# An attention block with adaptive layer norm: the order of the side work, one piece in each even step

## What is computed

```
h = _layernorm(x, axis=-1) * (1 + ca) + sa
x = x + ga * _L0_attn_ref(h, Wq, Wkv_down, Wk_up, Wv_up, Wo)
h = _layernorm(x, axis=-1) * (1 + cb) + sb
x = x + gb * _L0_ffn_ref(h, weight, disha)

# _L0_attn_ref(x):
q = (x @ Wq.T).reshape(b, t, N_HEADS, HEAD_DIM)
kv_latent = x @ Wkv_down.T
k = (kv_latent @ Wk_up.T).reshape(b, t, N_HEADS, HEAD_DIM)
v = (kv_latent @ Wv_up.T).reshape(b, t, N_HEADS, HEAD_DIM)
scores = jnp.einsum('bqhd,bkhd->bhqk', q, k) * scale
attn = jax.nn.softmax(scores, axis=-1)
out = jnp.einsum('bhqk,bkhd->bqhd', attn, v)
return out.reshape(b, t, N_HEADS * HEAD_DIM) @ Wo.T

# _L0_ffn_ref(x):
result = jnp.einsum('bsd,od->bso', x, weight)
pooled = x.reshape(*x.shape[:-1], x.shape[-1] // r, r).sum(axis=-2)
return result + pooled @ disha
```

## Time and profile before

| | us |
|---|---|
| median of 3 runs | 3562.01 (3559.07 to 3562.82) |
| profiled execution | 3557.84 |
| its span, first to last instruction | 3555.9 |
| PE busy | 3328.4 (94%) |
| POOL busy | 2510.2 (71%) |
| DVE busy | 2463.9 (69%) |
| ACT busy | 1672.1 (47%) |
| chain that ended last: PE, DVE, POOL, ACT | 74%, 9%, 6%, 3% |

### The profile page before, as it was taken

The page is one execution under the profiler, slowest core; times in us unless marked ns, Lnnn a source line. Parts: engine busy times, 40 slices in busy tenths (PEclk is TensorE's granted clock), DMA queues, the critical chain, the costliest instruction groups (busy, mean ns, idle before and its releaser), DMA issues.

```text
span 3555.9 us, 50728 instructions
## 1 busy us (share of the span) xinstructions
PE 3328.4 (94%) x14886; PEld 1920.0 (54%) x14886; DVE 2463.9 (69%) x2846; ACT 1672.1 (47%) x3075; POOL 2510.2 (71%) x1513
## 2 busy tenths in 40 slices
PE   5899999989999999999999999999999989999996
PEld 3444555545555564555646555464555645556454
DVE  4667767677676766767777676775767767676663
ACT  1444545444454444545444454544545445454443
POOL 1667677767776677667777677777777776777775
PEclk7999999999999999999999999999999999999998
DMA  1001010010101001010010100101010010100101
GB/s 56 30 24 51 22 59 20 28 49 30 52 19 62 21 25 51 28 55 19 31 50 22 60 20 28 48 31 52 19 62 19 28 53 24 54 25 28 36 30 33
DMA packets 98083, 129.34 MB, mean 36 GB/s; under 512 B 11121, under 2 KB 62449, under 8 KB 97777
## 3 DMA queue, kind: packets, MB, share of 16 engines
q1 hardware_dynamic: 97776, 125.64, 10.2%
...
## 4 chain that ended last, share of the span: by engine, by line
PE 74%; DVE 9%; issue 8%; POOL 6%; ACT 3%; DMA 0%; POOLq 0%; ACTq 0%; DVEq 0%; SPq 0%
PE ps_mix L544 22%; PE ps_max L587 12%; PE ps_score L565 12%; PE ps_score L567 10%; PE ps_side_b L532 5%; PE ps_side_b L649 5%; DVE neg_max L972 4%; POOL prob_sum L833 3%; PE ps_side_a L636 3%; PE ps_side_b L667 3%; DVE recip L952 2%; POOL x_in L852 1%; POOL rstd L819 1%; DVE h_lo L994 1%; ACT h_whole L772 1%
## 5 line engine op out<-in xcount | busy, mean ns | idle before, releaser
L833 POOL TENSOR_TENSOR prob_sum<-prob_sum,probs 128x1024 f32<-128x1024 f32 x768 | 1837.7, 2393 | 436.5 <-ACT probs L732 387.5
L972 DVE TENSOR_REDUCE neg_max<-ps_max 128x1 f32<-128x1024 f32 x1016 | 1240.8, 1221 | 694.4 <-PE ps_max L587 690.5
L732 ACT ACTIVATE probs<-ps_score 128x512 f32<-128x512 f32 x2048 | 1114.4, 597 | 1260.8 <-PE ps_score L567 1249.7
L544 PE MATMUL ps_mix<-probs,values 128*64 128x512 f32 x4096 | 994.6, 606 | 0.0
L565 PE MATMUL ps_score<-query,key_hi 128*128 128x512 f32 x2048 | 887.5, 433 | 46.6 <-issue 30.2
L567 PE MATMUL ps_score<-query_m,key_lo 128*128 128x512 f32 x2048 | 813.3, 397 | 0.0
L587 PE MATMUL ps_max<-key_hi,query 128*128 128x512 f32 x2032 | 669.7, 411 | 65.9 <-DVE neg_max L972 65.7
L565 PEld LDWEIGHTS ps_score<-query,key_hi 128*128 128x128 f32 x2048 | 387.6, 189 | 545.3 <-issue 409.9
L833 POOL TENSOR_TENSOR prob_sum<-probs 128x1024 f32<-128x1024 f32 x128 | 303.4, 2370 | 506.4 <-ACT probs L732 506.3
L544 PEld LDWEIGHTS ps_mix<-probs,values 128*64 128x64 f32 x4096 | 249.2, 136 | 481.1 <-issue 481.1
L952 DVE RECIPROCAL recip<-recip 128x128 f32<-128x128 f32 x512 | 481.5, 942 | 27.3 <-ACT recip L783 27.3
(11 more groups left out here) (115 smaller groups left out, 2725.8 us busy)
## 6 DMA issues: line engine op xcount, KB each, us to landing
query_m<-query SPq DMA_DIRECT2D x128, 512.0 KB, 3.2
...
query_m<-max_row SPq DMA_DIRECT2D x128, 4.0 KB
mixed<-in_L_wmod_dram SPq DMA_DIRECT2D x1, 1536.0 KB, 10.3
...
```

The source lines that it names most:

```text
L544: last = nc.tensor.matmul(ps_mix[g % 2][j * R:j * R + R, :], values[par][:, k, :], probs[:, s % RING, j * HALF:(j + 1) * HALF], start=(k = ...
L732: nc.scalar.activation(probs[:, s % RING, half * HALF:(half + 1) * HALF], ps_score[half], ACT.Exp, scale=SCALE).then_inc(exps_done, 1)
L833: nc.gpsimd.tensor_tensor(out=total[:, :], in0=before, in1=probs[:, s % RING, :], op=ALU.add).then_inc(adds_done, 1)
L972: nc.vector.tensor_reduce(neg_max[:, m:m + 1], z.max_bank(m, ps_max, ps_scores)[:, :], AX_X, ALU.max, negate=True).then_inc(maxima_done, 1)
```

## The change

`step_of` takes its numbers from a table, `PLAN`. The output projection of a chunk of 256 tokens is cut in two pieces of 128 tokens (8 pieces instead of 4, `NT` instead of `CHUNKS` in `BANK_B`), each with its own drain and statistics. In the plan every even step has one piece: queries 4 to 7 in steps 0, 2, 4, 6 of the next slot and 0 to 3 in 34, 44, 54, 60, `norm_t` in 8 to 14, `latent` in 20 and 22, `values_t` in 30 and 58. Before, in the groups where they had their turn, an output projection stood in the first step, a query in the third, `ffn` in the fifth and `norm2_t` in the seventh. `mixed_lo` has moved from steps 18, 26, 34, 42 to 13, 21, 35, 45, and the statistics, the normalisation and the gated weights are some steps earlier.

```diff
-STATS_STEPS = (2, 2, 3, 4, 8, 8, 9, 9)
-APPLY_STEPS = (6, 10)
+STATS_STEPS = (2, 2, 3, 3, 4, 5, 6, 7)
+APPLY_STEPS = (5, 8)
...
-GATE_STEPS = ((1, 13), (3, 16), (7, 17))
+GATE_STEPS = ((1, 11), (3, 14), (7, 15))
...
+PLAN = {
+    "query": (34, 44, 54, 60, STEPS, STEPS + 2, STEPS + 4, STEPS + 6),
+    "norm_t": (8, 10, 12, 14),
+    "latent": (20, 22),
+    "values_t": (30, 58),
+    "mixed_hi": (12, 20, 34, 44),
+    "mixed_lo": (13, 21, 35, 45),
+    "out_proj": (16, 18, 24, 28, 38, 40, 48, 50),
+    "norm2_t": (26, 36, 46, 56),
+    "h2_split": (27, 37, 47, 57),
+    "ffn": (32, 42, 52, 62),
+}
...
-        "norm_t": (10, 12, 14, 15)[i % 4],
-        "latent": 15 + 2 * i,
-        "values_t": 20 + 2 * i,
-        "query": NT * (i + 2) + 2,
         "max_row": STEPS - 4 + NT * i,
         "denominator": NT * (i + 1) + 3,
-        "mixed_hi": 18 + NT * i,
-        "mixed_lo": 18 + NT * i,
-        "out_proj": 24 + NT * i,
-        "norm2_t": 30 + NT * i,
-        "h2_split": 31 + NT * i,
-        "ffn": 36 + NT * i,
...
-    "out_proj": (8, 9, 11, 14),
+    "out_proj": (8, 8, 9, 9, 11, 11, 14, 14),
...
+                        g, j = divmod(i, CT)
+                        need(pe, mixed_split, CHUNKS * b + g + 1)
...
-                        for j in range(CT):
-                            for q, (mp, wp, p) in enumerate(products):
-                                last = nc.tensor.matmul(side[:, j * D:(j + 1) * D], mp[:, p, j * P:(j + 1) * P],
-                                                        wp[:, p, :], start=(q == 0), stop=(q == len(products) - 1))
+                        for q, (mp, wp, p) in enumerate(products):
+                            last = nc.tensor.matmul(side[:, 0:D], mp[:, p, j * P:(j + 1) * P],
+                                                    wp[:, p, :], start=(q == 0), stop=(q == len(products) - 1))
...
+                            nc.vector.tensor_tensor(x_mid[g][:, j, :], ps_b[:, 0:D], x_mid[g][:, j, :], ALU.add).then_inc(b_drained, 1)
                             need(dve, b_drained, count + 1)
...
+                            nc.vector.bn_stats(stats2[g % 2][:, j, :], x_mid[g][:, j, :]).then_inc(stats2_steps, 1)
+                            need_alone(dve, stats2_steps, 2 * (NT * b + i) + 1)
+                            nc.vector.bn_aggr(moments2[g % 2][:, j, :], stats2[g % 2][:, j, :]).then_inc(stats2_steps, 1)
```

27 lines of the change are left out of this document (11 added, 16 removed).

## The result

The changed kernel takes 3605.76 us (median of 4 runs, 3604.10 to 3613.59), the kernel before 3560.54 on the same chip: a ratio of 1.0133, 95% interval 1.0114 to 1.0152. It is slower by 45 us.

The account below looks back on a forecast made before the run. TensorE, busy 94% of the span, was taken as the bound, leaving little beside its waits. With +3.0 us a slot, +42 over 14 loop slots, and -10 at the ends, 3557.8 became 3590; 8 in 10 from 3520 to 3625.

Parts of the forecast that it names:

- Steps 0 to 3, 4 to 7, 20 to 63: Stretches of a slot priced at 13.4 us (12.64 before), 6.3 + 6.2, and about 140.3 (142.1 before).
- The waits named for steps 47 and 57: Maxima waiting for DVE: step 47 by 1.2 us behind `mixed_lo` of step 45, step 57 by 0.8.
- The wait for `mod1`: Steps 8 and 9: ACT's transpose drain waits for POOL's `mod1` copy; 9.9 us, 4.7 of it wait, moved, not removed.
- Steps 10 and 11: This pair of steps was priced at 6.4 us.
- Steps 14 and 15: `mixed_lo` and `h_lo` meet POOL's additions, delaying step 14's reduction to 6.4 us into the step: 10.3 us for 5.2 of work.
- the coin's edge: Step 13: whether POOL's addition or DVE's `mixed_lo` starts first, 0.08 us apart in a walk of 25 us.
- Steps 16 and 17: First half projection in step 16 waits for `w_out_lo` and `w_ffn_lo`: 7.0 us for 6.3.
- The slot and the loop: A slot goes from 211.7 to 214.7 us, +3.0; over 14 loop slots +42.
- The ends: First reduction earlier -9.7 us, last slot's bank hand-overs +1.5, first and last batch -1.5; together -10.
- DVE first: Rival: in step 13 `mixed_lo` precedes POOL's addition; steps 14, 15 take 8.0 us; total 3558; chance 0.23.
- The cover wins: Rival: neither `mixed_lo` nor `h_lo` meets an addition, -1.7 us a slot; 3524, or 3492 with ACT's wait half hidden; chance 0.22.
- The clock falls in each slot: Rival: the 4.9 us wait before step 15's maximum lowers TensorE's clock, some 2.5 us a slot; 3625; chance 0.18.

Follow-up runs that it names:

- row_clear: Changed kernel with `mod1` copied in step 5, first `mixed` chunk in 8 and 9, gates in 10 to 12, third transposition in 13, fourth chunk in 42, 43: 3519.19 us.
- before_mod1_early: Kernel before the change, with POOL copying `mod1` in step 6, ahead of the first normalisation, instead of step 10: 3511.90 us, ratio 0.9858.
- mod1_early: Changed kernel with POOL copying `mod1` in step 5, ahead of the first normalisation, instead of step 8: 3569.19 us, ratio 1.0025.
- swapped: Changed kernel with `h_lo` ahead of `mixed_lo` on DVE where both fall in one step: 3584.97 us, ratio 1.0065.
- mixed_early: Changed kernel with the first chunk of `mixed_hi` moved from step 12 to 8 and its `mixed_lo` from 13 to 9: 3595.75 us, ratio 1.0094.
- short_adds: Changed kernel with POOL's additions of steps 11 to 15 cut from 1024 to 64 columns (doesn't compute the reference): 3552.72 us, ratio 0.9975.
- front_old: Changed kernel with the front of its plan (statistics, normalisation, transposes, gates, first `mixed` chunks) as before the change: 3543.99 us, ratio 0.9952.
- spread: Changed kernel with `mod1` copied in step 5 and statistics, second normalisation, gates, subtractions, third transposition and `mixed` chunks reordered, no two subtractions together: 3479.51 us, ratio 0.9771.
- spread_late: spread with the last `h_lo` moved from step 15 to 17 and `w_ffn_lo` from 17 to 25 (computation changed, not usable): 3433.26 us, ratio 0.9644.

## Why the prediction was right, and where its steps were not

The forecast was 3590 with a range of 3520 to 3625; 3605.8 came out. The direction and both places of the loss were right. That the sum came as near as 16 us is in part luck: the 3590 leaves out the lower clock, which costs some 2.8 us a slot, and has the wait for DVE in step 15 1.8 us too long; the two errors cancel in part. By its steps:

- **Steps 0 to 3, 4 to 7, 20 to 63.** 13.4, 6.3 + 6.2 and 140.3 forecast; 13.35, 6.32 + 6.27 and 140.27 measured. The prices of a query, a half projection and a bare pair, taken from distances between score matmuls, carried this part. The waits named for steps 47 and 57 are there (0.94 and 0.59 us in slot 8, forecast 1.2 and 0.8; the steps take 4.64 and 4.28 us), and moving one `mixed_lo` took the first of them away (`row_clear`).
- **The wait for `mod1`.** 9.9 forecast from the distances of the earlier trace rows, 10.00 measured. It was said to be moved, not removed, and `before_mod1_early` shows that it was in the kernel before, worth 48 us there. What the prediction didn't ask is why the copy stood where it stood.
- **Steps 10 and 11.** 6.4 forecast, 7.65 measured. This is the first term that was mis-sized: the wait ahead brings the clock down to the lower level (0.78 over these two steps), and `mod1_early`, where that wait is gone, gives 6.37. The rival on the clock had this mechanism, but for step 15 alone.
- **Steps 12 and 13.** 7.8 forecast, 7.72 measured.
- **Steps 14 and 15.** 10.3 forecast and 10.33 measured, but the number is right by a sum of two errors. POOL came on time: 14.35 us after step 10's first score forecast for the addition that `mixed_lo` would meet, 14.22 measured. DVE came to `mixed_lo` 1.3 us later than walked (15.72 instead of 14.43), since steps 10 and 11 were slower by the clock. So in this slot there was no coin's edge; POOL was first by 1.5 us, `mixed_lo` waited only for the rest of the addition, and the reduction of step 14 started 4.9 us into its step, not 6.4. TensorE waited 3.14 us instead of 4.9. What made up for it is the clock: in slot 1, the one where the clock stayed up in steps 14 and 15, they took 8.8, in 12 others 10.1 to 11.0. Slot 12, shown above, is the walk itself: steps 10 and 11 took 6.38, the addition began at 14.22 us and DVE came at 14.35 (14.35 and 14.43 forecast), the reduction started 6.27 us into its step, and TensorE waited 4.50. With the clock down behind that wait the two steps took 12.3, 2 us over the 10.3.
- **Steps 16 and 17.** 7.0 forecast, 6.4 measured: the long stop ahead of them had given DVE time for `w_out_lo`. `swapped`, `mixed_early` and `short_adds`, which took the stop away, brought this wait out at once.
- **The slot and the loop.** 214.7 forecast, 215.5 measured by medians. The 14 slots took 59.8 us more than before where +42 was forecast: 0.8 a slot more by the terms above (11 us), and some 0.5 a slot (7 us) that the medians don't show, slots with the lower clock for longer and the loop's restart. There the stall of the earlier trace rows has moved from step 0 to step 1 and is as long. DVE waits 6.35 us for nothing that the profile shows (`issue`), and TensorE for DVE:

```profile
2040.84 0.49 PE L571 MATMUL ps_score<-query,key_hi 128*128 128x512 f32 x1 [0.74 <-issue]
...
2047.52 1.22 DVE L978 TENSOR_REDUCE neg_max<-ps_max 128x1 f32<-128x1024 f32 x1 [6.35 <-issue]
...
2048.80 1.22 PE L593 MATMUL ps_max<-key_hi,query 128*128 128x512 f32 x2 [4.00 <-DVE neg_max L978]
```

- **The ends.** -10 forecast, about -4 measured: slot 0 starts 7.2 us earlier (-9.7 forecast), and the last two slots cost 3.1 more where I had +1.5 and a gain beside it.

**The rivals.** *DVE first* came in no slot of the changed kernel: in 13 of 14 the clock had held DVE back, and in slot 12 POOL was first by 0.1 us, so there it was the coin's edge of the forecast. In `mod1_early`, where steps 10 and 11 take 6.4 in all slots, `mixed_lo` is first in 7 of 14 (1.2 to 1.4 us long), and steps 14 and 15 take 6.5 to 9.8 in these, on both sides of the rival's 8.0. *The cover wins* is what `front_old` (-16 us) and `spread` (-81) show for other orders of the front part. For the changed order `short_adds` is nearest to its condition, no meeting with an addition in step 13, and takes 3552.7 where the rival had 3524: of the 1.8 us that its slot has over the rival's 210.0, 1.2 are the slower steps 10 and 11. *The clock falls in each slot* came true in kind: in its 14 loop slots the changed kernel spent 143 us at the lower level in 32 stretches, the kernel before 48 us in 7 (six where the loop starts again, one in step 12 of slot 5), `spread_late` 20 us in 6, all where the loop starts again. Its price was put at 2.5 us a slot behind step 15; it is about 1.3 in steps 10 and 11 and 1.5 in 14 and 15, and it fell behind waits of 2.7 and 3.1 us, where the prediction held a wait of 2.7 to be nearer to those behind which it stays up.

The Trainium skill, GPSIMD Engine Reference, section Specifications, was the rule by which the slot would get slower (shared SBUF interfaces of VectorE and GpSimd, contention for instructions with two SBUF inputs). `short_adds` and the changed kernel agree: the same `h_lo` takes 0.68 us without an addition and 2.86 with one. DVE's reciprocals, with one SBUF input, take 0.94 us beside additions and without, and the reductions, whose input is in PSUM, 1.22. Here whichever of the two had begun was let finish.
